# Three moves in the order of a chain of four residual layers: one weight split, half a product, the experts' product

## The chip, the cores and the metric

The kernel runs on one core of a Trainium2 chip. The metric is the device time of one execution in microseconds. Every execution launches the program once.

## What is computed

Four layers, each added to its input, on x of 64 batches x 32 rows x 512 numbers (2,048 rows of 512). Cut to what matters:

```python
# L0: gated MLP with an adapter of rank 16 chosen by batch
gate = x @ W_gate.T + 0.5 * (x @ A_gate[id].T) @ B_gate[id].T      # 512 -> 1376
up   = x @ W_up.T   + 0.5 * (x @ A_up[id].T)   @ B_up[id].T
act  = silu(gate) * up
x = x + act @ W_down.T + 0.5 * (act @ A_down[id].T) @ B_down[id].T # 1376 -> 512
# L1: rows of a batch mixed by a 32 x 32 matrix chosen by batch
x = x + einsum('bct,bcd->bdt', x, W1[cond])
# L2: a dense layer, and 8 experts of rank 16, the best two of each row weighted
base = x @ W.T
top2, ids = top_k(x @ Wr.T + 5 * one_hot(lang), 2)
gates = sum(one_hot(ids) * softmax(top2))
x = x + base + 2 * einsum('bter,bte,eor->bto', x @ A.T, gates, B)
# L3: as L1, with other matrices
x = x + einsum('bct,bcd->bdt', x, W3[cond])
```

## The kernel before

The 2,048 rows are 16 tiles of 128. Precision is kept by splitting: each float32 operand of a matmul is held as a high part (ScalarE casts it, `hi`) and a low part (VectorE subtracts the high part from the whole, `lo`, line 1126 for most of them), and `product` on TensorE makes three matmuls of each product: high by high, high by low, low by high (lines 1397 to 1399). A split thus passes ScalarE first and VectorE second. Both engines walk the same hand-written list, `lane_jobs`, in order; TensorE has its own hand-written order at the end of the program; SP and GpSimd issue transfers from their own lists. Semaphores tie the five together: a job's low part counts up `s_lo`, and TensorE waits for it.

**First half, L0.** It is worked in steps s = 0 to 47; a step is one tile i and one of three groups n of the 1,376 columns, and `ORDER` gives the first steps as (0,0), (0,1), (1,0), (0,2), (1,1), (1,2). A step has `gate(s)` and `up(s)` (four chunks of 128 input columns each, so twelve matmuls for 512 columns), then `adapters(s)`, which adds the adapter product and needs the split of step s's B: job `("b", s)`, tile `b_sel`. ScalarE and VectorE then form act (job `("gate", s)`); TensorE transposes it, it is split (job `("act", d)`, tile `act_hl`), and `down(d)` multiplies it by W_down. `down` of a tile's first group also needs the adapter matrices A for down, job `("adt", i)`, which go into the tile `wd_sb` beside W_down (jobs `("wd", f)`). B is gathered by GpSimd; before it loads the second group of W_down, SP waits until step 3's B has landed.

**Second half, L1 to L3.** Tile after tile, in the loop at the end of the TensorE program. `l2_base(i, 1)` and `l2_base(i, 0)` are the two halves of the product with W, Wr and the experts' A, twelve matmuls each, into the PSUM tile `l2_ps[i % 2]`. VectorE chooses the two experts (`route_top`, `route_weights`, `route_gates`, lines 1283 to 1306) and writes the weighted inner values `hg`. `transpose_hg(i - 1)` (line 1551) turns them, ScalarE and VectorE split them (`hgt_hl`, `s_hgtlo`), and `experts(i - 1)` adds their product with the experts' B to the base in `l2_ps[(i - 1) % 2]`, six matmuls of 256 columns. When it has ended (`s_l2`), ScalarE (`high_x3`, line 998) and VectorE (`low_x3`, line 1317) split the result into `x3_hl`. `l3(i - 2)` and `l1(i + 3)` are single products of other tiles. Since there are two `l2_ps` tiles, a tile's first product waits until the one before last is out:

```python
if t >= 2:
    pe.wait_ge(*((s_x3lo, t - 1) if t - 2 < PLAIN else x3_count(t - 2)))
    pe.wait_ge(s_hg, t - 1)
```

Up to t = 14 that is VectorE's `low_x3(t - 2)`; for t = 15 it is a copy on ScalarE. After `l3`, ScalarE copies its result (`copy_y`) and casts the next input of L1 (`high_x1`); GpSimd makes the low part of that (`low_x1`, line 862) for tiles up to 15. VectorE's `take_x2` ends a tile's work there and hands the tile after next to the DMA.

Of the kernel before, what the change touches and what calls it, by code (L numbers as in the profile page):

```python
# [49 lines left out]
HC = H // P  # L50
NT = ROWS // P
# [124 lines left out]
def wd_items(n):  # L176
    return [("wd", f) for f in pieces_of(n)]
# [47 lines left out]
def lane_jobs(s):  # L225

    if s <= FREE:
        w1u, w2g, w2u = wgu_items(1, 1), wgu_items(2, 0), wgu_items(2, 1)
        return {-1: first_items(),
                0: (wgu_items(1, 0) + [("at", 0)] + w1u[:2] + [("b", 0), w1u[2], ("tm", 0), w1u[3], ("t", 0), ("b", 1),
                    ("tc", 0), w2g[0], ("gate", 0), w2g[1], ("at", 1)]),
                1: w2g[2:] + [("gate", 1), ("tm", 1)] + w2u[:2] + [("t", 1)] + w2u[2:] + [("tc", 1)],
                2: [("b", 2), ("adt", 0), ("b", 3), ("adt", 1), ("gate", 2), ("act", 0)] + wd_items(0),
                3: [("gate", 3)] + wd_items(1) + [("act", 1), ("b", 4)],
                4: wd_items(2) + [("act", 2), ("gate", 4), ("bd", 0), ("b", 5), ("x", 2, 0)],  # L240
                5: [("tdm", 0), ("td", 0), ("act", 3), ("x1", 0), ("at", 2), ("gate", 5), ("b", 6)],
                6: [("act", 4), ("tm", 2), ("t", 2), ("adt", 2), ("gate", 6), ("b", 7)]}[s]
    i, n = divmod(s, NC)
    last = [("act", s - 1)] if s - 1 not in MOVED else []
    if i == NT:
        return last + [("bd", i - 1), ("tdm", i - 1), ("td", i - 1), ("x1", i - 1)]
    acts = ([("act", s - 2)] if s - 2 in MOVED else []) + last
    if n == 0:
        return [("tm", i)] + acts + [("t", i), ("gate", s), ("b", s + 1)]
    if n == 1:  # L250
        x = [("x", i + 1, 0)] if i + 1 < NT else []
        return acts + x + [("bd", i - 1), ("gate", s), ("tdm", i - 1), ("b", s + 1), ("td", i - 1)]
    jobs = acts[:1] + [("x1", i - 1)] + acts[1:]
    if i + 1 < NT:
        return jobs + [("at", i + 1), ("gate", s), ("b", s + 1), ("adt", i + 1)]
    return jobs + [("gate", s)]
# [6 lines left out]
def bass_conditioned_residual_chain(nc, x_t, x_rows, it_cond, it_lang, wgu, wd, a_all, a_gu, a_d, b_d,  # L263
# [6 lines left out]
    with ExitStack() as ctx:  # L270
# [54 lines left out]
        act = sb("act", [2, H], F32, mem_a)  # L325
# [1068 lines left out]
        def _(pe):  # L1394
# [22 lines left out]
            def gate(s, c0, c1):  # L1417
                i, n = ORDER[s]
                out_ = gate_of(s) if n or i < 2 else bank(s, 0)[:, 0:AW + GATE0]
                if c0 == 0 and slot_before(s) is not None:  # L1420
                    pe.wait_ge(s_mul, slot_before(s) + 1)
                if c0 == 0 and n == 0 and i >= 1:
                    pe.wait_ge(s_lo, s_lo_of(("x", i, 0)))
                if c0 == 0 and n == 0 and i >= 2:
                    pe.wait_ge(s_lo, s_lo_of(("at", i)))
                for c in range(c0, c1):
                    if i == 0:
                        pe.wait_ge(s_lo, s_lo_of(("wgu", n, 0, c)))
                        if n == 0 and c % 2 == 0:
                            pe.wait_ge(s_lo, s_lo_of(("x", 0, c // 2)))  # L1430
                    mm = product(out_, x_of(i, c), gate_moving(i, n, c), c == 0, False)
                if n == 0 and i >= 2 and c1 == HC:
                    mm.then_inc(s_tx, 1)
# [42 lines left out]
            def down(d):  # L1476
                i, n = divmod(d, NC)
                pe.wait_ge(s_lo, s_lo_of(("act", d)))
                if d == 0:
                    pe.wait_ge(s_mul, step_of(1, 0) + 1)  # L1480
                if n == 0:
                    pe.wait_ge(s_lo, s_lo_of(("adt", i)))
                    if i >= 1:
                        pe.wait_ge(s_x1, i)
                at = i % 2 * AD_HALF
                for j, f in enumerate(pieces_of(n)):
                    w = cw(f)
                    if i == 0:
                        pe.wait_ge(s_lo, s_lo_of(("wd", f)))
                    a_hl = [act_hl[0:w, d % 2, part, j, :] for part in range(2)]  # L1490
                    for half in range(2):
                        mm = product(down_ps[:, half, 0:D_COLS], a_hl,
                                     [wd_sb[0:w, f, part, half, at:at + D_COLS] for part in range(2)],
                                     n == 0 and j == 0, False)
                mm.then_inc(s_d, 1)
# [30 lines left out]
            def l2_base(t, half, c0=0, c1=HC):  # L1526

                if half == 1:
                    pe.wait_ge(s_x2tlo, t + 1)
                    if t == 0:  # L1530
                        pe.wait_ge(s_mul, STEPS)
                    if t == 1:
                        pe.wait_ge(s_x1, NT)
# [3 lines that stand above are left out]
                for c in range(c0, c1):  # L1537
                    if t == 0 and half == 1:
                        pe.wait_ge(s_wlo, c + 1)
                    x_hl = x2t_hl[:, t % 2, 0, c, :], x2t_hl[:, t % 2, 1, c, :]  # L1540
                    at, w = half * L2_WIDTH[0], L2_WIDTH[half]
                    mm = product(l2_ps[t % 2][:, half, 0:w], x_hl,
                                 [w2ra_hl[:, part, c, at:at + w] for part in range(2)], c == 0, c == HC - 1)
                if c1 == HC:
                    mm.then_inc((s_base, s_logits)[half], 1)
# [33 lines left out]
            def whole(part, s):  # L1579
                part(s, 0, HC)  # L1580
# [20 lines left out]
            adapters(2)  # L1601
            adapters(3)
            gate(4, HC // 2, HC)
            down(0)
            transpose_act(1)
            whole(up, 4)
            down(1)
            transpose_act(2)
            adapters(4)
# [13 lines left out]
            for s in range(FREE + 1, STEPS):  # L1623
                i, n = ORDER[s]
# [31 lines left out]
            l1(3)  # L1656
            for i in range(1, NT - 2):
                l2_base(i, 1)
                transpose_hg(i - 1)
                if i + 1 < MOVED_X2:  # L1660
                    transpose_x2(i + 1)
                l2_base(i, 0, 0, HC // 2)
                experts(i - 1)
                l2_base(i, 0, HC // 2, HC)
                if i >= 2:
                    l3(i - 2)
                if i + 3 < NT:
                    l1(i + 3)
            l2_base(NT - 2, 1)
            transpose_hg(NT - 3)  # L1670
            l2_base(NT - 2, 0, 0, HC // 2)
            experts(NT - 3)
            l2_base(NT - 2, 0, HC // 2, HC)
            l2_base(NT - 1, 1)
            transpose_hg(NT - 2)
            l3(NT - 4)
# [70 lines left out]
```

## Time and profile before

| | |
|---|---|
| median of 3 runs | 550.65 us (550.13 to 554.97) |
| the profiled execution | 551.23 us, of which its span 549.4 us |
| TensorE busy | 539.2 us, 98% of the span |
| VectorE, ScalarE, GpSimd busy | 60%, 38%, 39% |
| DMA | 105.71 MB, 192 GB/s in the mean |
| granted TensorE clock | 1.00 in the mean (2.4 GHz) |

Busy is the time in which an engine had an instruction at work, so the highest share shows the engine that all others feed. Matmuls overlap: each starts when the one before has given up the array, and its recorded duration reaches beyond the start of the next. The spacing of starts is therefore what a matmul costs, and "idle before" is counted from the end of the one before. The two halves of the program lie at about 6 to 450 us and 450 to 547 us of the span.

### The profile page before, as it was taken

The page shows a single profiled execution, that of the slowest core. Times are in us where ns is not written, and L with a number is a line of the kernel's source. Part 1 is how long each engine was busy: PE and PEld are TensorE (multiplying, and loading weights), DVE is VectorE, ACT ScalarE, POOL GpSimd, SP SyncE. Part 2 cuts the span into 40 slices and gives each one's busy share as a digit, 9 for nine tenths or more (in the row PEclk, how much of TensorE's full clock was granted, in tenths as well). Part 3 has the DMA queues.
Part 4 walks back from the last instruction along what each step waited for, and adds up shares of the span by engine and source line. Part 5 has one row for each costly group of instructions (what it writes and reads, how often), then busy time and mean ns, then how long its engine had stood idle before and what let it go on. Part 6 is the DMA issues. An engine that isn't in the chain of part 4 may idle for free.

```text
span 549.4 us, 8715 instructions
## 1 busy us (share of the span) xinstructions
PE 539.2 (98%) x3120; PEld 488.5 (89%) x3120; DVE 330.6 (60%) x775; ACT 209.7 (38%) x418; POOL 212.8 (39%) x236
## 2 busy tenths in 40 slices
PE   5999999999999999999999999999999999999997
PEld 5879989898989898989898989898989899999996
DVE  5788554645564646564555455545554577777765
ACT  6675242424242424242333323232323543444432
POOL 4743244746584757433232323241412342121100
PEclk9999999999999999999999999999999999999999
DMA  8985555666667666655555555564555832667642
GB/s 287 374 254 201 163 180 177 190 209 197 207 199 221 184 219 190 229 171 190 161 179 164 177 164 177 163 184 161 186 164 169 299 116 92 214 212 227 229 140 76
DMA packets 73466, 105.71 MB, mean 192 GB/s; under 512 B 9552, under 2 KB 40912, under 8 KB 73424
## 3 DMA queue, kind: packets, MB, share of 16 engines
q1 hardware_dynamic: 62400, 67.87, 37.6%
q0 software_dynamic: 10880, 37.23, 22.2%
q8 instruction: 24, 0.39, 0.3%
q14 instruction: 18, 0.15, 0.1%
q10 hardware_dynamic: 144, 0.06, 0.0%
HBM read 78.39 MB, written 26.74 MB: 191 GB/s over the span
## 4 chain that ended last, share of the span: by engine, by line
PE 96%; DVE 2%; DMA 1%; ACT 1%; issue 0%; SPq 0%; DVEq 0%; ACTq 0%
PE gu_ps L1397 15%; PE gu_ps L1399 15%; PE gu_ps L1398 15%; PE down_ps L1397 9%; PE down_ps L1398 9%; PE down_ps L1399 9%; PE l_ps L1397 5%; PE l_ps L1398 5%; PE l_ps L1399 5%; PE gu_ps L1404 3%; PE gu_ps L1405 3%; PE down_ps L1405 1%; PE down_ps L1404 1%; DMA wg_sb_raw<-wgu 1%; PE act_t L1473 0%; DVE wd_sb L1126 0%
## 5 line engine op out<-in xcount | busy, mean ns | idle before, releaser
L798 POOL DMA_INDIRECT b_sel_raw<-b_gu,idx_rank x48 | 46.3, 965 | 153.3 <-PE gu_ps L1405 135.2
L1397 PE MATMUL down_ps<-wd_sb,act_hl 128*128 128x288 f32 (+1 forms) x352 | 103.9, 295 | 0.3 <-DVE wd_sb L1126 0.3
L1398 PE MATMUL down_ps<-wd_sb,act_hl 128*128 128x288 f32 (+1 forms) x352 | 103.7, 295 | 0.0
L1399 PE MATMUL down_ps<-wd_sb,act_hl 128*128 128x288 f32 (+1 forms) x352 | 103.6, 294 | 0.0
L1397 PE MATMUL gu_ps<-w_sb,xt 128*128 128x512 f32 x256 | 101.1, 395 | 0.2 <-DVE act L1199 0.2
L1399 PE MATMUL gu_ps<-w_sb,xt 128*128 128x512 f32 x256 | 100.0, 391 | 0.0
L1398 PE MATMUL gu_ps<-w_sb,xt 128*128 128x512 f32 x256 | 100.0, 391 | 0.0
L1199 DVE TENSOR_TENSOR act<-act,gu_ps 128x512 f32<-128x512 f32 (+1 forms) x47 | 29.8, 634 | 106.7 <-ACT act L926 106.7
L926 ACT ACTIVATE act<-gu_ps 128x512 f32<-128x512 f32 (+1 forms) x47 | 26.2, 556 | 176.9 <-PE gu_ps L1405 176.9
L798 POOL DMA_INDIRECT a_raw<-a_all,idx_batch x60 | 70.2, 1170 | 54.0 <-DVE wd_sb L1126 39.9
L1397 PEld LDWEIGHTS down_ps<-wd_sb,act_hl 128*128 128x128 f32 (+1 forms) x352 | 66.0, 188 | 2.2 <-DVE wd_sb L1126 0.7
L1398 PEld LDWEIGHTS down_ps<-wd_sb,act_hl 128*128 128x128 f32 (+1 forms) x352 | 66.1, 188 | 1.2
L1399 PEld LDWEIGHTS down_ps<-wd_sb,act_hl 128*128 128x128 f32 (+1 forms) x352 | 66.0, 188 | 0.0
L1399 PEld LDWEIGHTS gu_ps<-w_sb,xt 128*128 128x128 f32 x256 | 48.1, 188 | 10.6
L1397 PEld LDWEIGHTS gu_ps<-w_sb,xt 128*128 128x128 f32 x256 | 48.1, 188 | 9.0 <-DVE act L1199 0.6
L1398 PEld LDWEIGHTS gu_ps<-w_sb,xt 128*128 128x128 f32 x256 | 48.2, 188 | 8.2
L1126 DVE TENSOR_TENSOR b_sel<-b_sel_raw,b_sel 128x1024 fp32r<-128x1024 f32 (+1 forms) x48 | 52.2, 1088 | 3.4 <-ACT b_sel L901 3.3
L862 POOL TENSOR_TENSOR x_hl<-x,x_hl 128x512 fp32r<-128x512 f32 x16 | 21.8, 1360 | 67.9 <-ACT x_hl L1032 67.9
L901 ACT CAST b_sel<-b_sel_raw 128x1024 fp32r<-128x1024 f32 (+1 forms) x48 | 45.7, 952 | 0.9 <-DMA b_sel_raw<-b_gu,idx_rank 0.9
L1397 PE MATMUL l_ps<-w2ra_hl,x2t_hl 128*128 128x328 f32 (+1 forms) x128 | 41.6, 325 | 0.0
L1398 PE MATMUL l_ps<-w2ra_hl,x2t_hl 128*128 128x328 f32 (+1 forms) x128 | 39.8, 311 | 0.0
L1399 PE MATMUL l_ps<-w2ra_hl,x2t_hl 128*128 128x328 f32 (+1 forms) x128 | 39.5, 309 | 0.0
(165 smaller groups left out, 1057.6 us busy)
## 6 DMA issues: line engine op xcount, KB each, us to landing
act_blocks<-act SPq DMA_DIRECT2D x41, 256.0 KB, 4.2
x_res<-act_blocks SPq DMA_DIRECT2D x164, 64.0 KB
xt_raw<-x_t SPq DMA_DIRECT2D x16, 256.0 KB, 5.0
w_sb_raw<-wgu SPq DMA_DIRECT2D x16, 256.0 KB, 7.9
x_res<-x_rows SPq DMA_DIRECT2D x16, 256.0 KB, 2.8
x_after_l<-x_res SPq DMA_DIRECT2D x16, 256.0 KB, 2.2
bd<-bd_hl SPq DMA_DIRECT2D x16, 256.0 KB
x<-x_after_l SPq DMA_DIRECT2D x16, 256.0 KB, 2.9
```

The lines of the kernel that those rows point to most:

```text
L798: nc.gpsimd.indirect_dma_start(out=dst, out_offset=None, in_=table, in_offset=bass.IndirectOffsetOnAxis(ap=idx, axis=0)).then_inc(s, 16)
L862: pool.tensor_tensor(x1_hl[:, t % 2, 1, :], x1[:, t % 2, :], x1_hl[:, t % 2, 0, :].bitcast(F32), ALU.subtract).then_inc(s_x1lo, 1)
L901: sc.copy(out_, in_).then_inc(s_hi, 1)
L926: sc.activation(act_of(s), gate_of(s), ACT.Silu).then_inc(s_silu, 1)
L1126: return ve.tensor_tensor(out_, raw, high.bitcast(F32), ALU.subtract)
L1199: ve.tensor_tensor(a, a, up_of(s), ALU.mult).then_inc(s_mul, 1)
L1397: pe.matmul(out_, stationary[0], moving[0], start=start, stop=False, skip_group_check=True)
L1398: pe.matmul(out_, stationary[0], moving[1], start=False, stop=False, skip_group_check=True)
L1399: return pe.matmul(out_, stationary[1], moving[0], start=False, stop=stop, skip_group_check=True)
L1404: pe.matmul(out_, stationary, moving[0], start=False, stop=False, skip_group_check=True)
L1405: return pe.matmul(out_, stationary, moving[1], start=False, stop=True, skip_group_check=True)
```

## The change

The arithmetic, the transfers and the number of instructions stay the same. Three orders change.

```diff
@@ lane_jobs @@
-                2: [("b", 2), ("adt", 0), ("b", 3), ("adt", 1), ("gate", 2), ("act", 0)] + wd_items(0),
+                2: [("b", 2), ("b", 3), ("adt", 0), ("adt", 1), ("gate", 2), ("act", 0)] + wd_items(0),
@@ the order on TensorE, first half @@
             gate(4, HC // 2, HC)
+            up(4, 0, HC // 2)
             down(0)
             transpose_act(1)
-            whole(up, 4)
+            up(4, HC // 2, HC)
             down(1)
@@ the order on TensorE, second half @@
             for i in range(1, NT - 2):
                 l2_base(i, 1)
+                l2_base(i, 0, 0, 1)
                 transpose_hg(i - 1)
                 if i + 1 < MOVED_X2:
                     transpose_x2(i + 1)
-                l2_base(i, 0, 0, HC // 2)
+                l2_base(i, 0, 1, HC)
                 experts(i - 1)
-                l2_base(i, 0, HC // 2, HC)
                 if i >= 2:
                     l3(i - 2)
                 if i + 3 < NT:
                     l1(i + 3)
             l2_base(NT - 2, 1)
+            l2_base(NT - 2, 0, 0, 1)
             transpose_hg(NT - 3)
-            l2_base(NT - 2, 0, 0, HC // 2)
+            l2_base(NT - 2, 0, 1, HC)
             experts(NT - 3)
-            l2_base(NT - 2, 0, HC // 2, HC)
```

On VectorE, in the work of step 2, around 34 us (`b_sel` of 704 columns is step 2's B, of 1024 columns step 3's; `wd_sb<-a_raw` is a tile's A for down, in two halves):

```order
 L1126 TENSOR_TENSOR b_sel<-b_sel_raw,b_sel 128x704 [waits s_hi]
-L1126 TENSOR_TENSOR wd_sb<-a_raw,wd_sb 128x11x32 [waits s_hi]
-L1126 TENSOR_TENSOR wd_sb<-a_raw,wd_sb 128x11x32
-L1126 TENSOR_TENSOR b_sel<-b_sel_raw,b_sel 128x1024 [waits s_hi]
+L1126 TENSOR_TENSOR b_sel<-b_sel_raw,b_sel 128x1024 [waits s_hi]
+L1126 TENSOR_TENSOR wd_sb<-a_raw,wd_sb 128x11x32 [waits s_hi]
+L1126 TENSOR_TENSOR wd_sb<-a_raw,wd_sb 128x11x32
```

Step 3's B now stands ahead of the first tile's A; ScalarE's casts stand likewise.

On TensorE, behind the last gate product of step 4, around 38 us (`gu_ps_1` is the up product, `down_ps` the down product of the first tile):

```order
 L1399 MATMUL gu_ps_0<-w_sb,xt 128x512
+L1397 MATMUL gu_ps_1<-w_sb,xt 128x512
+L1398 MATMUL gu_ps_1<-w_sb,xt 128x512
+L1399 MATMUL gu_ps_1<-w_sb,xt 128x512
+L1397 MATMUL gu_ps_1<-w_sb,xt 128x512
+L1398 MATMUL gu_ps_1<-w_sb,xt 128x512
+L1399 MATMUL gu_ps_1<-w_sb,xt 128x512
 L1397 MATMUL down_ps<-wd_sb,act_hl 128x288 [waits s_lo,s_mul]
```

The six up products are taken out behind the transpositions that follow the down product.

On TensorE, in a tile of the second half. Between the transposition of hg and the experts' product (`l_ps<-b_hl,hgt_hl`) two chunks of the base product stood before:

```order
 L1551 MATMUL hgt_ps<-ident_sb,hg 128x128
 L1397 MATMUL l_ps<-w2ra_hl,x2t_hl 128x320
 L1398 MATMUL l_ps<-w2ra_hl,x2t_hl 128x320
 L1399 MATMUL l_ps<-w2ra_hl,x2t_hl 128x320
 L1397 MATMUL l_ps<-w2ra_hl,x2t_hl 128x320
 L1398 MATMUL l_ps<-w2ra_hl,x2t_hl 128x320
 L1399 MATMUL l_ps<-w2ra_hl,x2t_hl 128x320
 L1397 MATMUL l_ps<-b_hl,hgt_hl 128x256
```

and now three:

```order
 L1551 MATMUL hgt_ps<-ident_sb,hg 128x128
 L1397 MATMUL l_ps<-w2ra_hl,x2t_hl 128x320
 L1398 MATMUL l_ps<-w2ra_hl,x2t_hl 128x320
 L1399 MATMUL l_ps<-w2ra_hl,x2t_hl 128x320
 L1397 MATMUL l_ps<-w2ra_hl,x2t_hl 128x320
 L1398 MATMUL l_ps<-w2ra_hl,x2t_hl 128x320
 L1399 MATMUL l_ps<-w2ra_hl,x2t_hl 128x320
 L1397 MATMUL l_ps<-w2ra_hl,x2t_hl 128x320
 L1398 MATMUL l_ps<-w2ra_hl,x2t_hl 128x320
 L1399 MATMUL l_ps<-w2ra_hl,x2t_hl 128x320
 L1397 MATMUL l_ps<-b_hl,hgt_hl 128x256
```

The first chunk of the half now stands ahead of the transposition, and the two chunks that followed the experts' product stand before it; behind the experts' product comes `l3(i - 2)` at once.

## Rows read from the trace of the kernel before

**Rows 1.** The page's first part: busy us, share of the span, instructions.
```profile
PE 539.2 (98%) x3120; PEld 488.5 (89%) x3120; DVE 330.6 (60%) x775; ACT 209.7 (38%) x418; POOL 212.8 (39%) x236
```

**Rows 2.** Timeline, TensorE, 35 to 44 us: start, duration, instruction [idle before <-releaser].
```profile
35.45 0.50 PE L1404 MATMUL gu_ps<-b_sel,t_hl 128*128 128x512 f32 x1 [0.74 <-DVE b_sel L1126]
...
37.63 0.39 PE L1399 MATMUL gu_ps<-w_sb,xt 128*128 128x512 f32 x1
38.29 0.37 PE L1397 MATMUL down_ps<-wd_sb,act_hl 128*128 128x288 f32 x1 [0.27 <-DVE wd_sb L1126]
...
41.10 0.48 PE L1397 MATMUL gu_ps<-w_sb,xt 128*128 128x512 f32 x1
...
43.93 0.29 PE L1397 MATMUL down_ps<-wd_sb,act_hl 128*128 128x288 f32 x1
```

**Rows 3.** Timeline, SP's transfers, ScalarE and VectorE, 32 to 43 us.
```profile
32.10 5.16 SPq L680 DMA_DIRECT2D wd_sb_raw<-wd  x8
...
32.31 0.87 ACT L905 CAST wd_sb<-a_raw 128x352 fp32r<-128x352 f32 x2
33.08 1.06 ACT L901 CAST b_sel<-b_sel_raw 128x1024 fp32r<-128x1024 f32 x1
...
33.25 0.96 DVE L1126 TENSOR_TENSOR wd_sb<-a_raw,wd_sb 128x352 fp32r<-128x352 f32 x2
34.17 1.23 DVE L1126 TENSOR_TENSOR b_sel<-b_sel_raw,b_sel 128x1024 fp32r<-128x1024 f32 x1
...
42.27 0.68 DVE L1126 TENSOR_TENSOR act_hl<-act_t,act_hl 128x512 fp32r<-128x512 f32 x1
```

**Rows 4.** Timeline, TensorE, a tile of the second half and the next's start.
```profile
469.15 0.31 PE L1397 MATMUL l_ps<-w2ra_hl,x2t_hl 128*128 128x328 f32 x1
...
470.95 0.27 PE L1551 MATMUL hgt_ps<-ident_sb,hg 128*128 128x128 f32 x1
...
471.94 0.35 PE L1397 MATMUL l_ps<-b_hl,hgt_hl 128*128 128x256 f32 x1
...
472.60 0.28 PE L1399 MATMUL l_ps<-b_hl,hgt_hl 128*128 128x256 f32 x1
472.72 0.31 PE L1397 MATMUL l_ps<-w2ra_hl,x2t_hl 128*128 128x320 f32 x1
...
473.61 0.39 PE L1397 MATMUL l_ps<-x_hl,bd_hl 128*128 128x512 f32 x1
...
474.99 0.31 PE L1397 MATMUL l_ps<-w2ra_hl,x2t_hl 128*128 128x328 f32 x1
```

**Rows 5.** Timeline, VectorE, the same tile: the subtraction that frees the bank.
```profile
473.60 0.69 DVE L1317 TENSOR_TENSOR x_hl<-l_ps,x_hl 128x512 fp32r<-128x512 f32 x1 [0.19 <-ACT x_hl L998]
```

**Rows 6.** Timeline, starts of tile 2 and of tile 14, the latter with its releaser.
```profile
462.83 0.39 PE L1397 MATMUL l_ps<-w2ra_hl,x2t_hl 128*128 128x328 f32 x1
...
532.04 0.69 DVE L1317 TENSOR_TENSOR x_hl<-l_ps,x_hl 128x512 fp32r<-128x512 f32 x1 [0.20 <-ACT x_hl L998]
...
532.84 0.39 PE L1397 MATMUL l_ps<-w2ra_hl,x2t_hl 128*128 128x328 f32 x1
```

**Rows 7.** Timeline, TensorE, the transposition of hg in tile 2.
```profile
465.05 0.33 PE L1551 MATMUL hgt_ps<-ident_sb,hg 128*128 128x128 f32 x1 [0.19 <-DVE hg L1306]
```

**Rows 8.** Timeline, VectorE's gate arithmetic and GpSimd's subtraction, tiles 2 and 3.
```profile
462.64 1.29 POOL L862 TENSOR_TENSOR x_hl<-x,x_hl 128x512 fp32r<-128x512 f32 x1 [5.64 <-ACT x_hl L1032]
463.02 0.92 DVE L1295 TENSOR_TENSOR route<-route 128x1 f32<-128x1 f32 x1
...
474.58 0.16 DVE L1295 TENSOR_TENSOR route<-route 128x1 f32<-128x1 f32 x1
...
475.30 0.17 DVE L1302 TENSOR_TENSOR route<-route 128x8 f32<-128x8 f32 x1
475.50 0.29 DVE L1306 TENSOR_TENSOR hg<-l_ps,route 128x128 f32<-128x128 f32 x1
...
475.69 1.30 POOL L862 TENSOR_TENSOR x_hl<-x,x_hl 128x512 fp32r<-128x512 f32 x1 [4.38 <-ACT x_hl L1032]
```

## Prediction

> **What bounds the kernel now.** I read the page first: TensorE is busy for 539.2 of 549.4 us [rows 1]. Nearly all that is not busy lies before the first product and in the tail, so the rest of the work was read in two narrow stretches of the timeline, for each of which I noted at what time a product starts, what it waited for, and when the result it needs was there.
>
> The first stretch is 34 to 44 us. TensorE waits 0.74 us at 35.45 for step 3's B [rows 2]; VectorE's subtraction of that B runs from 34.17 for 1.23 us, to 35.40 [rows 3], so the adapter products start 0.05 after it. At 38.29 the first down product waits for a piece of W_down [rows 2]. The second stretch is the last 100 us, the sixteen tiles of the second half. Call the start of a tile's first product (`l2_base(i, 1)`) S. In an ordinary tile S is 469.15 and the next tile's is 474.99: 5.84 us [rows 4]. TensorE has no idle time there, but it has little slack either. That start needs a PSUM bank which the tile before last left: experts(i-1) ends, ScalarE casts the bank (`high_x3`), VectorE subtracts (`low_x3`, line 1317), and only then `s_x3lo` lets `l2_base(i+1, 1)` begin. The last of the six experts products starts at 472.60 [rows 4], the subtraction 1.00 later at 473.60, and it takes 0.69, to 474.29 [rows 5]. So the bank is free 0.70 us ahead of 474.99.
>
> How long TensorE needs after a release is seen where it comes last. The subtraction at 532.04 ends at 532.73 and the product starts at 532.84, 0.11 later, and takes 0.39 where its like takes 0.31 at 469.15 [rows 4, 6]; so 0.11 and then about 0.07 more. The second tile's start at 462.83 is of the same kind (0.39) [rows 6]: no slack at all there.
>
> **The change in the first stage.** Nothing is added or removed; two items trade places on ScalarE and VectorE, and six of the twelve up products of step 4 go ahead of down(0).
>
> B ahead of A: step 3's B has landed by 32.10, where SP's wait for it ends [rows 3]. ScalarE is free for its cast at 32.31, where it casts A now; the cast takes 1.06, to 33.37. VectorE is free at 33.25 and subtracts from 33.41 to 34.64. The adapters start at 34.69 instead of 35.45: 0.76 gained. The work behind on VectorE is the same in sum, but starts 0.11 later for the wait on the cast.
>
> Half an up product ahead of down(0): the last gate product before it starts at 37.63, its slot ends 0.23 later at 37.86; minus 0.76 is 37.10. Twelve up products take 2.83 (41.10 to 43.93) [rows 2], six 1.38. So down(0) can start at 38.48, and its weights, there for 38.29 now and 0.11 later then, are in time. From down(0) to down(1) it is 5.64 now; less the 0.08 of a restart and the six products that is 4.18, so down(1) could start at 42.66. But down(1) also needs the activations' low part: VectorE's subtraction at 42.27 takes 0.68 [rows 3], to 42.95, with the 0.11 to 43.06. TensorE starts at 43.17 in place of 43.93, and loses 0.08 on the first product. **Gain 0.68.** The wait has moved from B and W_down to the activations, where VectorE's queue, which nothing shortens, is the bound. The ends: 0 if the B isn't there early, 1.27 (43.93 - 42.66) if the activations were no bound. I take 0.68, since VectorE is unbroken there. After 44 us TensorE has all its inputs early, so this gain is kept.
>
> **The change in the second stage.** Experts(i-1) goes behind all twelve products of `l2_base(i, 0)`, and the transposition of hg behind the first three. What each tile has afterwards, from S:
> - `l2_base(i, 1)`: 1.80 (469.15 to 470.95), plus 0.07 if S was a restart
> - three products: 0.44 (six take 0.89, 472.72 to 473.61)
> - transposition: 0.10 (470.95 to 471.94 is 0.99, less the six products' 0.89)
> - nine products: 1.33
> - to the start of the last experts product: 0.59 (five spacings of 0.12). Now it is 0.66 (471.94 to 472.60), since the first experts product just meets its operand; with nine products between, this 0.07 goes.
>
> All from [rows 4]. The last experts product thus starts at S + 4.33 instead of S + 3.45. To this come 1.00, 0.69 and 0.11 [rows 5, 6]: the next S cannot be before S + 6.13. TensorE's own work is 5.84 - 0.07 + 0.07 = 5.84, so a wait of 0.29 us stands where there was 0.70 of slack. This is **+0.29 for each of the ten starts** of tiles 4 to 13: +2.9.
>
> Other starts, one by one. Tile 2 (462.83) has no slack, six products go in front of its releaser: +0.89. Tile 3: TensorE waited 0.19 there for hg (465.05) [rows 7] and the tile lasted 6.32 (462.83 to 469.15); now 6.13: -0.19. Tile 14 (532.84), before which no `l1` stands, is at its release already: +0.88. Tile 15 has neither `l1` nor `l3` in front of it; its releaser is ScalarE's copy; I price it as tile 14, +0.88. Behind it the tail is as before. **Sum of the stage: 2.9 + 0.89 - 0.19 + 0.88 + 0.88 = +5.36.**
>
> Who else is moved? GpSimd. ScalarE's copy of y and cast of x1 follow `l3`, and GpSimd's subtraction follows them. `l3` starts at 473.61, GpSimd at 475.69 [rows 4, 8], 2.08 later, and takes 1.30. Call the start of the last experts product L. Now `l3` is at L + 0.12, so GpSimd runs from L + 2.20 to L + 3.50. VectorE's gate arithmetic follows the bank's subtraction (L + 1.00): line 1295 stands 0.98 behind it (474.58), so L + 1.98 to 2.14, just ahead of GpSimd; line 1302 (475.30) at L + 2.70, in the middle of it; hg (475.50) 0.20 after that [rows 8]. In the trace an operation of VectorE that meets GpSimd is held to its end: line 1295 at 463.02 takes 0.92 instead of 0.16 and ends at 463.94, GpSimd's ends at 463.93 [rows 8]. So line 1302 is held to L + 3.50, and hg is there at L + 3.70 + 0.29 = L + 3.99. The next transposition wants it at L + 1.80 + 1.87 + 0.44 = L + 4.11. It just fits: cost nothing, cover 0.12.
>
> The Trainium skill (SBUF — State Buffer, Who interferes with whom) says that a VectorE instruction with two SBUF inputs contends with a GpSimd instruction that reads SBUF, and the row at 463.02 agrees (0.92 against 0.16 us). It says further that copies, casts and `tensor_scalar` can take the shared ports too. No row here shows that for a wide one. By that the two operations between lines 1295 and 1302 would be held as well, and the cover of 0.12 would be gone: that is the second rival below.
>
> **Sum.** -0.68 + 5.36 = +4.68. The profiled execution took 551.23 us (span 549.4); it would be 555.9 and its span 554.1. The median of the three runs is 550.65, 0.58 lower: **555.3**.
>
> **The rivals.**
> 1. The release isn't late (other side). Everything does what was meant: -0.68, the 0.19 of the wait on hg, 0.07 in twelve tiles: -1.7, 548.9 us. It decides where the bank is free by the time TensorE wants it: experts end 0.82 later against a slack of 0.70, so the ScalarE-VectorE chain would have to be 0.12 to 0.29 shorter than the 1.69 that it shows [rows 4, 5], and at tiles 2, 14 and 15 even 0.9 shorter. Against it: these durations repeat from tile to tile. 0.06.
> 2. VectorE is held longer by GpSimd, so hg becomes the bound. If line 1295 is caught (it clears by 0.06), the transposition comes as at 465.05, 1.12 after GpSimd's end at 463.93 [rows 7, 8], at L + 4.62 against L + 4.11: 0.51 for each of the nine tiles in which GpSimd still subtracts, +4.6, 559.9 us. If only the `tensor_scalar` operations are, half: +2.3, 557.6. For it: margins of 0.06 and 0.12; against it: the distances are fixed by the same release. 0.16.
> 3. B isn't there at 32.31. It landed only 0.2 before [rows 3]. If it comes 0.8 later the gain of the first stage is gone: +5.36, 556.0 us. 0.10.
>
> **How the numbers follow.** Mine holds 0.68, at 554.3 to 556.4 by itself: 0.08, the price of one restart, either way at each of the thirteen starts. The range takes in the third rival and the milder form of the second: 553.0 to 558.0; outside are the first (0.06), the full form of the second (0.07) and a rest. One per cent, 5.5 us, is about what a measurement of this kernel can tell from no change. Over 556.2 lie the second rival (0.16), some of the third and of mine (0.12 together): slower 0.28. Under 545.1 nothing leads; TensorE is at work 98% of the span [rows 1]: 0.02. Same: 0.70.
>
> **What would show it.** In the timeline after: adapters of step 3 at 34.7 without idle, down(0) at 38.5, and a wait of down(1) on VectorE's `act_hl` of some 0.3 to 0.5. In the table of waits a new row at the top, TensorE `l_ps` L1397 waiting for VectorE `x_hl` L1317, in 13 tiles, some 0.1 to 0.9 each, and tiles 6.13 apart instead of 5.84. Line 1302 at about 1 us instead of 0.17. Were TensorE to wait for hg (L1306) at line 1551 instead, the second rival is right; were there no wait in the second stage, the first. My sum is wrong if the chain from experts to the release is not the 1.80 of now, or if a tile's x2 blocks, which VectorE now hands to the DMA later in a tile, come too late.

## The result, and the profile after

The changed kernel took **558.29 us** (median of ten executions, 557.59 to 561.92), against 555.25 us for the kernel before (ten executions, 550.13 to 556.76) in the same comparison: a ratio of **1.0097, interval 1.0063 to 1.0132**. The prediction was 555.3 us in a range of 553.0 to 558.0, so the time lies 0.3 us above the range. The 555.25 needs a remark: four of its ten executions lie at 550 to 552 us and six at 555 to 557 us, while in three later comparisons the median of before was 551.25, 552.02 and 551.57 us. Against those the change costs 6.3 to 7.0 us (1.1 to 1.3%), though they ran at other times and on three different chips. What can make one execution 4 us longer than the next is found at the end, in the trace of e7_mid. Executions over 1.5% above the quickest of the same kernel (one of e9_mid_release took 1085.72 us) are in the medians and not in the ratios.

The profiled execution took 557.59 us, its span is 555.8 us (before 549.4). The page's first line of TensorE, which answers to [rows 1], and its chain that ended last:

```profile
PE 542.3 (98%) x3120; PEld 486.2 (87%) x3120; DVE 340.1 (61%) x775; ACT 210.7 (38%) x418; POOL 209.8 (38%) x236
...
PE 87%; DVE 4%; POOL 3%; DMA 3%; issue 2%; ACT 1%; SPq 0%; ACTq 0%; DVEq 0%
```

VectorE is busy 9.5 us more (340.1 against 330.6) with the same 775 instructions. There aren't more of them, so some must have become longer. That is the first sign that GpSimd stands in VectorE's way.

I noted the start S of each tile's first product (128x328) in both traces; the difference from one tile to the next:

| stretch into tile | before, us | after, us | difference | forecast |
|---|---|---|---|---|
| 2 | 5.59 | 6.48 | +0.89 | +0.89 |
| 3 | 6.32 | 6.07 | -0.25 | -0.19 |
| 4 to 12 (nine) | 5.84 to 5.85 | 6.29 to 6.46 | +4.77 in sum | +2.6 |
| 13 | 5.84 | 6.13 | +0.29 | +0.29 |
| 14 | 5.25 | 6.13 | +0.88 | +0.88 |
| 15 | 4.53 | 5.33 | +0.80 | +0.88 |
| tile 1 to tile 15 | 80.13 | 87.51 | **+7.38** | +5.36 |

Tile 1 itself starts 1.02 us earlier than before (456.22 against 457.24), and 7.38 - 1.02 = 6.36 is the growth of the span but for 0.04.

The timeline of TensorE after, a tile and the next one's start, answers to [rows 4]:

```profile
468.77 0.39 PE L1397 MATMUL l_ps<-w2ra_hl,x2t_hl 128*128 128x328 f32 x1
...
471.19 0.33 PE L1551 MATMUL hgt_ps<-ident_sb,hg 128*128 128x128 f32 x1
...
472.68 0.28 PE L1397 MATMUL l_ps<-b_hl,hgt_hl 128*128 128x256 f32 x1
...
473.27 0.28 PE L1399 MATMUL l_ps<-b_hl,hgt_hl 128*128 128x256 f32 x1
473.39 0.40 PE L1397 MATMUL l_ps<-x_hl,bd_hl 128*128 128x512 f32 x1
...
475.06 0.39 PE L1397 MATMUL l_ps<-w2ra_hl,x2t_hl 128*128 128x328 f32 x1
```

The last experts product starts at S + 4.50 (forecast 4.33), and `l3` 0.12 behind it. ScalarE and VectorE free the bank as before; these rows answer to [rows 5]:

```profile
473.65 0.58 ACT L998 CAST x_hl<-l_ps 128x512 fp32r<-128x512 f32 x1 [0.80 <-PE l_ps L1399]
474.26 0.69 DVE L1317 TENSOR_TENSOR x_hl<-l_ps,x_hl 128x512 fp32r<-128x512 f32 x1 [0.57 <-ACT x_hl L998]
```

From 473.27 to 474.26 it is 0.99, the subtraction ends at 474.95, and TensorE starts 0.11 later at 475.06: the release chain of the forecast (1.00 + 0.69 + 0.11), to 0.01 us. The start itself is a restart (0.39 instead of 0.31). What is new is the 0.17 ahead of it: the transposition of hg at 471.19 takes 0.33, the mark of a late operand. The waits of TensorE after say the same (engine, output, line, releaser: us in total, times, longest):

```profile
PEld l_ps L1397 <- issue: 7.7, 13, 1.2
...
PEld hgt_ps L1551 <- DVE hg L1306: 2.5, 9, 0.4
...
PE l_ps L1397 <- issue: 1.8, 3, 0.8
```

The wait for the bank stands where it was forecast, but the table puts it down to "issue", not to the subtraction of line 1317. Of the thirteen in the first row twelve are starts of tiles 2 to 9 and 11 to 14, and one is tile 1, which waits 0.21 us before the change too; tile 10 is in the third row. It has to be seen by the times themselves: in each of tiles 2 to 14 the start is 0.10 or 0.11 behind the subtraction's end. And nine transpositions wait for hg, which was forecast for none.

Why hg is late, in the tile that starts at 468.77 and in a later one:

```profile
468.79 0.62 ACT L1032 CAST x_hl<-x 128x512 fp32r<-128x512 f32 x1 [0.16 <-DMA x<-x_after_l]
...
469.35 0.29 DVE L1301 TENSOR_SCALAR route<-head_sb,route 128x8 f32<-128x8 f32 x1
...
469.49 1.30 POOL L862 TENSOR_TENSOR x_hl<-x,x_hl 128x512 fp32r<-128x512 f32 x1 [5.74 <-ACT x_hl L1032]
469.67 1.14 DVE L1302 TENSOR_TENSOR route<-route 128x8 f32<-128x8 f32 x1
470.84 0.29 DVE L1306 TENSOR_TENSOR hg<-l_ps,route 128x128 f32<-128x128 f32 x1
...
481.93 1.36 DVE L1301 TENSOR_SCALAR route<-head_sb,route 128x8 f32<-128x8 f32 x1
481.98 1.29 POOL L862 TENSOR_TENSOR x_hl<-x,x_hl 128x512 fp32r<-128x512 f32 x1 [4.90 <-ACT x_hl L1032]
```

GpSimd's subtraction and VectorE's gate arithmetic now lie on top of each other. At 469.67 it is line 1302 that is held (1.14 us, before 0.17 in [rows 8]); at 481.93 it is line 1301, a `tensor_scalar` of 128x8 (1.36 us instead of 0.29). Both end 0.02 us after GpSimd's instruction; the one at 463.02 in [rows 8] ended 0.01 after it. Of the nine tiles three have line 1302 held (the next start 6.29 to 6.32 us on) and six line 1301 (6.37 to 6.46).

In the first half, after, the rows that answer to [rows 2, 3]:

```profile
31.98 1.05 ACT L901 CAST b_sel<-b_sel_raw 128x1024 fp32r<-128x1024 f32 x1 [0.42 <-DMA b_sel_raw<-b_gu,idx_rank]
33.07 1.23 DVE L1126 TENSOR_TENSOR b_sel<-b_sel_raw,b_sel 128x1024 fp32r<-128x1024 f32 x1 [0.58 <-ACT b_sel L901]
34.35 0.51 PE L1404 MATMUL gu_ps<-b_sel,t_hl 128*128 128x512 f32 x1 [0.48 <-DVE b_sel L1126]
...
42.79 0.40 PE L1397 MATMUL down_ps<-wd_sb,act_hl 128*128 128x288 f32 x1 [0.28 <-DVE act_hl L1126]
```

The wait has moved to `act_hl` at down(1), as forecast, and down(1) starts 1.14 us earlier than before. Most of that is not the change's doing (below).

### The profile page after: what moved, and what is told of

It is laid out like the page before. It is cut to its first block, busy times and chain, and to the rows that moved or that the text cites. A ratio compares the mean times of both kernels' runs of the same rounds, so it can differ in the third digit from the quotient of the medians.

```text
span 555.8 us, 8715 instructions
## 1 busy us (share of the span) xinstructions
PE 542.3 (98%) x3120; PEld 486.2 (87%) x3120; DVE 340.1 (61%) x775; ACT 210.7 (38%) x418; POOL 209.8 (38%) x236
## 4 chain that ended last, share of the span: by engine, by line
PE 87%; DVE 4%; POOL 3%; DMA 3%; issue 2%; ACT 1%; SPq 0%; ACTq 0%; DVEq 0%
PE gu_ps L1397 13%; PE gu_ps L1399 13%; PE gu_ps L1398 13%; PE down_ps L1397 8%; PE down_ps L1398 8%; PE down_ps L1399 8%; PE l_ps L1397 5%; PE l_ps L1398 4%; PE l_ps L1399 4%; PE gu_ps L1404 3%; PE gu_ps L1405 3%; POOL a_raw L798 2%; DVE wd_sb L1126 1%; DMA b_sel_raw<-b_gu,idx_rank 1%; DMA x_landed<-x_blocks 1%
## 5 line engine op out<-in xcount | busy, mean ns | idle before, releaser
L798 POOL DMA_INDIRECT a_raw<-a_all,idx_batch x60 | 68.6, 1144 | 54.0 <-DVE wd_sb L1126 39.6
```

Source lines behind the costliest of these rows:

```text
L798: nc.gpsimd.indirect_dma_start(out=dst, out_offset=None, in_=table, in_offset=bass.IndirectOffsetOnAxis(ap=idx, axis=0)).then_inc(s, 16)
```

## The experiments

For each profile the time from the start of tile 1 to that of tile 15 is given, since it is free of what happens in the first half; before the change it is 80.13 us. The ratios are against the kernel before, run beside on the same chip.

**e1_first: only the two moves in the first half.**

```diff
-                2: [("b", 2), ("adt", 0), ("b", 3), ("adt", 1), ...
+                2: [("b", 2), ("b", 3), ("adt", 0), ("adt", 1), ...
+            up(4, 0, HC // 2)
             down(0)
             transpose_act(1)
-            whole(up, 4)
+            up(4, HC // 2, HC)
```

> Only the two moves of the first half (step 3's B split ahead of the first tile's A; half of step 4's up product ahead of the first down); second half as before. My account: both traces show TensorE waiting for B (0.74 us before, 0.48 after, B's DMA landing 0.42 late for ScalarE after) and the rest of the gain is 0.2 to 0.7 us, so this kernel is 0.2 to 0.7 us faster than before and nothing in the second half moves (tile starts 5.84 apart). Rival: the first half's moves cost something (DMA or queue effects), and the kernel is slower than before by 0.5 us or more.

Measured: 552.06 us, ratio 1.0014 [0.9972, 1.0056]. Tile 0 starts at 446.74 instead of 447.36, 0.62 earlier. The adapters of step 3 start at 34.66 (forecast 34.69) and down(0) at 38.42 (38.48), neither with an idle time before it in the record, and down(1) starts at 43.16 (43.17), with the wait that was named:

```profile
43.16 0.40 PE L1397 MATMUL down_ps<-wd_sb,act_hl 128*128 128x288 f32 x1 [0.29 <-DVE act_hl L1126]
```

The tiles of the second half stand 5.84 and 5.85 apart as before; tile 1 to 15 is 80.09. So the first half does what its step says, by 0.6 to 0.7 us in the trace. The times can't confirm it: the median is 0.8 us higher than that of before, and the interval is 4.6 us wide.

**e2_second: only the move of the experts' product and the transposition**, with the first half as before (the loop as in the diff of the change).

> Only the second half's move (first chunk ahead of the transposition of hg, experts behind all base products); first half as before. My account: the whole loss is here: +7 us from the second tile's start on against a trace of before (6.13 apart without GpSimd's meeting, 6.3 to 6.45 with it), so 6 to 8 us slower than a quick run of before. Rival: the first half carries part of the loss; then this kernel is less than 4 us slower than e1_first.

Measured: 560.17 us, ratio 1.0150 [1.0098, 1.0202]. Tile 1 to 15 took 88.25 us, +8.12. It is this part that costs. Against the 551.25 us of before the median is 8.9 us higher, where 6 to 8 were expected; three of its six executions lie at 558.2 to 558.4 and three at 561.9 to 564.6, and the profiled one, 561.93, has a wait of 2.01 us in the first half. The second half is 0.7 us worse than in the full change, and half of that is one tile, which took 6.78 us (the same tile in the full change 6.42):

```profile
515.16 0.62 ACT L982 CAST x2t_hl<-x_landed 128x512 fp32r<-128x512 f32 x1 [1.56 <-DMA x_landed<-x_blocks]
...
515.79 0.57 ACT L998 CAST x_hl<-l_ps 128x512 fp32r<-128x512 f32 x1
...
516.50 0.68 DVE L1317 TENSOR_TENSOR x_hl<-l_ps,x_hl 128x512 fp32r<-128x512 f32 x1
...
517.28 0.39 PE L1397 MATMUL l_ps<-w2ra_hl,x2t_hl 128*128 128x328 f32 x1 [0.55 <-issue]
517.44 1.29 POOL L862 TENSOR_TENSOR x_hl<-x,x_hl 128x512 fp32r<-128x512 f32 x1 [5.07 <-ACT x_hl L1032]
517.47 1.27 DVE L1295 TENSOR_TENSOR route<-route 128x1 f32<-128x1 f32 x1
```

The last experts product starts at 515.06. ScalarE waits 1.56 us for the DMA of x2, the cast that begins the release is queued behind that one, and the subtraction starts 1.44 us after the last experts product instead of 0.99. The last two rows show line 1295 held whole by GpSimd, the case which the forecast saw clear by 0.06 us. Behind tile 2, where it is held before the change too, this happens once, and the tile that it delays (517.28 to 523.72) took 6.44 us, no more than those with line 1301 held.

**e3_poollate: the changed kernel, with GpSimd's subtraction held back until hg is written.** Nothing else moves; VectorE's gates then never meet it.

```diff
             def low_x1(t):
                 pool.wait_ge(s_x1hi, t + 1)
+                if t >= 5:
+                    pool.wait_ge(s_hg, t - 3)
```

> The changed kernel, with GpSimd's subtraction of x1 (low_x1, tiles 5 to 15) held until the tile's hg is written, so that it can't meet VectorE's gate arithmetic. Theory A (VectorE held by GpSimd makes hg late in ten tiles): lines 1301 and 1302 fall back to 0.2 to 0.3 us, tiles 3 to 13 are 6.13 apart throughout, and the kernel is 2.0 to 2.2 us faster than the changed one. Theory B (only the bank's release counts; the extra over 6.13 has another cause, such as late x2 blocks from the DMA): the gate lines become short but the spacing stays 6.3 to 6.45, time unchanged within 0.5.

Measured: 556.04 us, ratio 1.0074 [1.0042, 1.0106]; span 554.1 us, tile 1 to 15 85.23 us. Every tile from 4 to 14 now stands 6.11 to 6.13 us from the one before. The rows of a tile:

```profile
469.61 0.28 DVE L1303 TENSOR_SCALAR route<-head_sb,route 128x8 f32<-128x8 f32 x1
469.93 0.17 DVE L1304 TENSOR_TENSOR route<-route 128x8 f32<-128x8 f32 x1
470.13 0.29 DVE L1308 TENSOR_TENSOR hg<-l_ps,route 128x128 f32<-128x128 f32 x1
...
470.56 1.28 POOL L864 TENSOR_TENSOR x_hl<-x,x_hl 128x512 fp32r<-128x512 f32 x1 [4.77 <-DVE hg L1308]
```

(The edit shifts the line numbers by two.) Line 1302, here 1304, takes its 0.17 us again. Without the meeting tile 1 to 15 is thus 87.51 - 85.23 = **2.28 us** shorter. In the changed kernel 2.16 of these lie ahead of the last experts product, where hg is waited for; 0.12 is one release (at 513.36) behind a late DMA of x2, which in e3_poollate comes in time. What is left over before, 85.23 - 80.13 = 5.10 us, is put down to the bank; the early release below tests it.

**e4_same: the kernel before, once more**, for the spread.

> The kernel before, unchanged, to see its own spread and a second trace of it: its ten runs lie in two groups, near 551 and near 556 us. If the groups are a matter of the order of events within the kernel, a trace near 556 shows tiles of the second half over 5.84 apart or waits that the first trace has not; if they come from outside (the moment at which TensorE's clock rises, the chip), the tiles are 5.84 apart and the time sits elsewhere.

Measured: 551.33 us (550.49 to 557.66), ratio 1.0005 [0.9973, 1.0037]. Its second half repeats to 0.01 us a tile (tile 3 to 0.05), tile 1 to 15 in 80.09. What this execution took more, 1.0 us, lies in the first half: a down product waits 1.28 us for `act_hl` at 185.84, where the trace of [rows 1] has no such wait. It isn't one of the executions near 556 us, so it says nothing of those.

**e5_release: the changed kernel, with the bank given back early.** VectorE copies the finished base from PSUM to SBUF (`x3`) in one instruction, this alone releases the bank, and ScalarE and VectorE make the high and low parts from the copy. It adds an instruction of 0.68 us to each tile and takes the cast and the subtraction out of TensorE's way. GpSimd is left as in the changed kernel.

```diff
+            def raw_x3(t):
+                ve.wait_ge(s_l2, t + 1)
+                ve.tensor_copy(halves(x3[:, t % 3, :], 0, H), base_of(t, 0, H)).then_inc(s_x3raw, 1)
...
-                low_x3(i - 1)
+                raw_x3(i - 1)
                 route_weights(i)
                 route_gates(i)
+                low_x3(i - 1)
...
-                        pe.wait_ge(*((s_x3lo, t - 1) if t - 2 < PLAIN else x3_count(t - 2)))
+                        pe.wait_ge(*((s_x3raw, t - 1) if t - 2 < PLAIN else x3_count(t - 2)))
```

> The changed kernel, with the bank let go earlier: VectorE first copies the tile's result from PSUM to SBUF, TensorE's next product in the bank waits for that copy alone, and ScalarE and VectorE split it from SBUF (VectorE's subtraction behind hg); one VectorE copy more per tile. GpSimd's subtraction stays where it is. Bank theory: the bank is free 1.1 us after the start of the last experts product instead of 1.8, TensorE's own work (5.77) is the bound, tiles 3 to 13 are 5.77 to 5.8 apart, hg is written before GpSimd starts, and the kernel takes 549.5 to 550.5, 8 us less than the changed one and 0.5 to 1.5 less than before. Rival (the order itself is slow, by hg or by the x2 blocks): the spacing stays at 6.1 or more and at least 4 us of the loss remain.

Measured: 553.41 us, ratio 1.0024 [0.9984, 1.0063]; the profiled execution 550.67 us with a span of 548.5. The 549.5 to 550.5 us that were expected are missed: six executions lie at 550.7 to 552.7 and six at 554.1 and more. The tiles up to 13 now stand 5.76 to 5.87 us apart (one 6.05), and tile 1 to 15 took 80.70 us, 6.81 less than the changed kernel. A tile's start, with the copy and GpSimd of this kernel:

```profile
478.22 0.68 DVE L1318 COPY x<-l_ps 128x512 f32<-128x512 f32 x1
...
479.10 0.39 PE L1405 MATMUL l_ps<-x_hl,bd_hl 128*128 128x512 f32 x1
479.32 0.31 PE L1403 MATMUL l_ps<-w2ra_hl,x2t_hl 128*128 128x328 f32 x1
```

The bank is free at 478.90 and wanted at 479.32; the product takes 0.31 again, no restart. The same edit also ends the meeting with GpSimd, in every tile: VectorE's gates now start right behind the 0.68 us copy, without the 0.6 us for ScalarE's cast, and hg has begun before GpSimd starts. So this run alone doesn't separate the two; e3_poollate and e6_release_poollate do. Tile 15, whose releaser is ScalarE's copy and not in the edit, stays at 5.33.

**e8_before_release: the kernel before, with the same early release.** The control.

> The kernel before, with the early release of the bank of e5_release and nothing else. Control: before has 0.70 us of slack at that wait, so by the bank theory the spacing stays at 5.84 and only the starts of tiles 2 and 14, which are at their release, gain about 0.1 each: same time as before within 0.5 us. If this is faster by over 1 us, e5_release proves nothing of the order.

Measured: 551.39 us, ratio 1.0004 [0.9966, 1.0043], most tiles 5.84 us apart (two of 5.98 and 6.04), tile 1 to 15 80.29. Where the release isn't the bound, giving it earlier brings nothing. The 6.8 us of e5_release are therefore the cure of what the change had made, and no gain of the early release itself.

**e6_release_poollate: the changed kernel with both cures.**

> The changed kernel with both cures: the bank released by VectorE's copy to SBUF, and GpSimd's subtraction held back behind hg. With the early release alone the tiles started 5.76 to 5.87 us apart. If the 0.09 us that some tiles kept came from GpSimd holding a gate line, they now start 5.76 us apart throughout, about 0.5 us less in sum: 550.5 us in an undisturbed execution, a ratio of 0.999 to 1.002. If the spread comes from something else (the base product's own late operand, or VectorE's copy ahead of the gates), the spacing stays mixed and the time with it.

Measured: 551.76 us, ratio 1.0008 [0.9974, 1.0041]; tile 1 to 15 80.66 us. From e3_poollate it differs by the early release alone, and takes 85.23 - 80.66 = **4.57 us** less: with GpSimd out of the way in both, this is what the late release costs, and the late DMA of one tile (below) hides another 0.46.

What was expected against e5_release is not shown. GpSimd starts 0.58 us behind hg in both (in e5_release 474.86 behind 474.28, here 475.75 behind 475.17), so holding it back there changed nothing. Ten of the eleven starts of tiles 3 to 13 stand 5.76 to 5.84 apart and one 6.23. In that one a DMA is late, ScalarE's cast of x2 with it, and VectorE's copy that frees the bank is queued behind its own part of that split:

```profile
507.42 0.62 ACT L985 CAST x2t_hl<-x_landed 128x512 fp32r<-128x512 f32 x1 [1.30 <-DMA x_landed<-x_blocks]
...
508.14 0.69 DVE L1264 TENSOR_TENSOR x2t_hl<-x_landed,x2t_hl 128x512 fp32r<-128x512 f32 x1 [0.87 <-ACT x2t_hl L985]
508.75 0.68 DVE L1320 COPY x<-l_ps 128x512 f32<-128x512 f32 x1
```

The copy starts 1.17 us after the last experts product instead of 0.34. It is the same in e5_release: in two tiles (5.85 and 5.87) the copy starts 0.80 and 0.82 after it, and three that begin with such a restart take 5.83 to 5.85. Once the release is early there is little slack towards that DMA.

**e7_mid: the experts' product behind three of the four chunks** (in tiles 1, 13 and 14 where it was before), with GpSimd held back and the first-half moves. The release chain starts three products (0.44 us) earlier than in the change.

```diff
+                first = 0 if i in (1, NT - 3) else 1
-                l2_base(i, 0, 0, 1)
+                l2_base(i, 0, 0, first)
                 transpose_hg(i - 1)
...
-                l2_base(i, 0, 1, HC)
+                l2_base(i, 0, first, 2 + first)
                 experts(i - 1)
+                l2_base(i, 0, 2 + first, HC)
```

> A compromise: the changed kernel with experts one chunk earlier (behind three of the four chunks), in tiles 1, 13 and 14 where it was before the change, and GpSimd's subtraction held until hg is written. By the bank theory the bank is free at 5.61 of a tile whose own work takes 5.77, so there is no wait: tiles 3 to 12 are 5.77 to 5.8 apart, and the kernel is 0.5 to 1.5 us faster than before, near 550.2. If a start needs more lead than 0.16 us the spacing is 5.84 and the kernel equals before.

Measured: 552.60 us, ratio 0.9993 [0.9957, 1.0028]. Most tiles stand 5.83 to 5.84 us apart, 5.24 and 4.53 at the end, 79.64 from tile 1 to 15: 0.49 less than before, 0.39 of it in tile 3. By moving back one chunk the whole loss is gone, but the 5.77 us per tile that were hoped for are not there.

**e9_mid_release: e7_mid with the early release.**

> This kernel puts together what the runs so far gave room for: both moves in the first half; the experts behind three of the four chunks of the base products (in tiles 1, 13 and 14 where they stood before); GpSimd's subtraction held back behind hg; and the PSUM bank of the base products given back by one VectorE copy to SBUF. If the 0.07 to 0.08 us that the order with three chunks kept (its tiles started 5.83 us apart) is the late release of the bank, the tiles now start 5.76 us apart, as most did with the early release, and the last two stretches stay at 5.24 and 4.53 us: about 79 us from the second tile's start to the last one's, 1.1 us under the kernel before, and 0.6 us less in the first half, so 549.5 us, a ratio of 0.997. If the 5.83 us come from something that the release doesn't touch (hg's transposition or the chain over line 1317), the spacing stays at 5.83 and the time at 550.5 us or within 0.2% of before.

Measured: 552.78 us, ratio 1.0022 [0.9988, 1.0056]. The spacing stays at 5.82 to 5.85 (two of 5.92), tile 1 to 15 in 79.51, and TensorE waits 1.07 us for step 3's B in this trace; the 549.5 us that were hoped for are missed. So the 0.07 over e5's 5.76 is not the release. The rows of TensorE in e9_mid_release say what it is:

```profile
482.11 0.27 PE L1559 MATMUL hgt_ps<-ident_sb,hg 128*128 128x128 f32 x1
...
483.10 0.35 PE L1405 MATMUL l_ps<-b_hl,hgt_hl 128*128 128x256 f32 x1
...
485.71 0.31 PE L1405 MATMUL l_ps<-w2ra_hl,x2t_hl 128*128 128x328 f32 x1
```

Between the transposition and the first experts product stand six products, as in [rows 4], and the experts' operand just comes in time: 0.35 as at 471.94 there. With nine products between, as in the changed kernel at 472.68, the same product takes 0.28. These are the 0.07 us per tile which the change does gain. They would come to 0.8 us of 551. e5_release keeps them and pays 1.22 us at the starts of tiles 2, 14 and 15 (5.87, 5.39 and 5.33 against 5.59, 5.25 and 4.53). Its order with the old one in tiles 1, 13 and 14 was not tried. None of the kernels beats the one before by an amount that the times can tell.

## Why the prediction was wrong, step by step

**The late release: right, in place and size.** "The next S cannot be before S + 6.13": 6.13 us into tiles 13 and 14 of the changed kernel, and 6.11 to 6.13 into all from 4 to 14 in e3_poollate. In the stretch into 14 GpSimd no longer subtracts; in the one into 13 it still does, but comes too late to hold anything:

```profile
527.05 0.17 DVE L1302 TENSOR_TENSOR route<-route 128x8 f32<-128x8 f32 x1
527.07 1.31 POOL L862 TENSOR_TENSOR x_hl<-x,x_hl 128x512 fp32r<-128x512 f32 x1 [5.20 <-ACT x_hl L1032]
```

e3_poollate against e6_release_poollate (4.57 us), with e8_before_release as the control, shows that it is this wait. The single starts were off by -0.06 (tile 3) and -0.08 (tile 15, whose releaser is ScalarE's copy and which I had priced as tile 14).

**"It just fits: cost nothing, cover 0.12": this step failed.** It cost 2.28 us (e3_poollate against the changed kernel), because the term that places GpSimd was wrong. GpSimd was put at L + 2.20, by its distance from `l3` in one row of before. With L = 473.27 it starts at 475.77, L + 2.50:

```profile
475.07 0.62 ACT L1032 CAST x_hl<-x 128x512 fp32r<-128x512 f32 x1 [0.20 <-DMA x<-x_after_l]
...
475.77 1.31 POOL L862 TENSOR_TENSOR x_hl<-x,x_hl 128x512 fp32r<-128x512 f32 x1 [4.98 <-ACT x_hl L1032]
475.96 1.14 DVE L1302 TENSOR_TENSOR route<-route 128x8 f32<-128x8 f32 x1
```

In the nine tiles with a meeting GpSimd starts at L + 2.28 to L + 2.58. ScalarE's cast ahead of it waits for the DMA that brings x; the record shows 0.16 to 0.23 us of it in three of the nine tiles and names nothing in the others. The one trace of before that the prediction had shows that wait nowhere, so no row had a price for it: the distance was carried over to a place where another input came last. e4_same, the kernel before once more, has one (0.26 us at 470.51); a second trace would have warned. The load of x is issued 0.43 us behind the transfer of VectorE's `take_x2`, which stands behind hg. Before, it was issued at 470.98 for a cast at 474.98, 4.00 us ahead; after, at 472.22 for the cast at 475.07, 2.85 ahead. By these rows a late hg makes the next load late, and with it GpSimd and the next hg; no run separates that.

Two smaller errors of the working nearly cancel. Line 1302's hand-over to hg was taken as 0.20 from its end, but in [rows 8] 0.20 is the distance of the two starts (475.30 and 475.50), and 0.03 that from the end: 0.17 too much. And from the end of hg to the transposition it takes 0.06 (471.13 to 471.19), which the cover left out. With both put right the cover would have been 0.23; GpSimd's 0.30 ate it. hg starts at 477.14 and is there at 477.43, L + 4.16 and not L + 3.99. In the tile that starts at 468.77 the transposition was wanted at S + 2.31 (1.87 and 0.44), 471.08; it starts at 471.19, 0.11 late, and its own restart makes the 0.17 by which the last experts product is behind S + 4.33.

The further error is the one that was named as open: the narrow `tensor_scalar` of line 1301 is held too (1.36 us), which makes tiles of 6.37 to 6.46 out of 6.29. That is the second rival in its milder form, 557.6 us with a chance inside 0.16. That the profiled execution took 557.59 is luck to the digit: the half in that rival was a guess, three of the nine tiles had line 1302 held, and not 1301, and the first half was off by 0.34. A cover of 0.12 us between two sums was no ground for five chances in six on "nothing".

**The first half: right in mechanism, with luck in the sum.** e1_first gives 43.16 for the forecast 43.17 and 0.62 us at tile 0. In the changed kernel's own trace step 3's B was 0.42 late (the third rival, partly), and TensorE was nonetheless 1.02 us ahead at tile 1. That is luck. It had been 0.85 ahead before the first changed instruction, which leaves 0.17 for the change in this trace and not 0.68: its first products stood 0.29 us apart until about 9 us of the span and 0.16 from there on, in the trace of before only from about 11 us. The same program does both.

**The sum.** The second half cost 2.02 more than forecast and the first half took 0.34 less: +1.68, which is the profiled 557.59 against my 555.9. The other 1.3 us up to 558.29 lie in the last step, "the median of the three runs is 0.58 lower": of the ten executions of the changed kernel the profiled one is the lowest, so subtracting went the wrong way (0.70 us up instead of 0.58 down).

**The chances.** "Slower by over 1%" had 0.28. The ratio in the first comparison is 1.0097; against the 551.25 us that before took beside the experiments it would be 1.013. With the failed step's 2.3 us the sum would have been 557.6, 1.3% above before, and that chance the larger one.

## What to carry to other kernels

Moving a product behind independent work gives its operand more time and takes it from whoever waits for its result: before the move, follow the result to the next use of its PSUM bank, and subtract the delay from the slack that is there (0.88 us later, against a slack of 0.70 less the 0.11 of a restart, cost 0.29 us in each of ten tiles). Where a step is found to fit by a tenth of a microsecond next to an engine that blocks another, put the failure's price into the sum and not into the rivals. And a distance between two instructions holds only as long as the same input comes last; whether it is read from start to start or from end to start has to stand beside it.

## What the runs showed of the hardware

**Who holds whom.** These VectorE instructions, with all their operands in SBUF, met GpSimd's subtraction and ended with it: 0.17 became 1.14 us (128x8 `tensor_tensor`), 0.29 became 1.36 (128x8 `tensor_scalar`), 0.16 became 1.27 (128x1 `tensor_tensor`), from the rows above. The `tensor_scalar` was held though it had started 0.05 us before GpSimd; the `tensor_tensor` at 527.05, 0.02 us before it, was not. The Trainium skill (SBUF — State Buffer, Who interferes with whom) has the `tensor_scalar` among those that can take shared ports; the row at 481.93 agrees, and also for one of eight columns. Not held was a `tensor_scalar` of one column, in the trace of before, inside GpSimd's 462.64 to 463.93 of [rows 8]:

```profile
462.65 0.14 DVE L1293 TENSOR_SCALAR route<-route 128x1 f32<-128x1 f32 x1
```

The other way round, GpSimd pays: where a wide subtraction of VectorE had begun before it, in e9_mid_release, VectorE keeps its 0.68 us and GpSimd takes 1.45 instead of 1.30:

```profile
480.75 0.68 DVE L1324 TENSOR_TENSOR x_hl<-x,x_hl 128x512 fp32r<-128x512 f32 x1
481.12 1.45 POOL L865 TENSOR_TENSOR x_hl<-x,x_hl 128x512 fp32r<-128x512 f32 x1 [4.37 <-ACT x_hl L1035]
```

**A late DMA, and the clock behind it.** e7_mid's profiled execution took 554.14 us, while its lowest five took 549.4 to 550.5. Its trace shows where:

```profile
130.52 0.40 ACT L1023 CAST bd_hl<-bd_raw 128x256 fp32r<-128x256 f32 x1 [5.90 <-DMA bd<-bd_hl]
130.83 0.61 ACT L903 CAST act_hl<-x_res 128x512 fp32r<-128x512 f32 x1
...
132.33 0.61 PE L1399 MATMUL down_ps<-wd_sb,act_hl 128*128 128x288 f32 x1 [2.77 <-DVE act_hl L1128]
132.74 0.44 PE L1400 MATMUL down_ps<-wd_sb,act_hl 128*128 128x288 f32 x1
132.98 0.44 PE L1401 MATMUL down_ps<-wd_sb,act_hl 128*128 128x288 f32 x1
```

ScalarE stands 5.90 us for a DMA (`bd`), the cast of the activations is queued behind it, and TensorE waits 2.77 us. Then the granted clock is 0.50 (1.2 GHz) in the stretch from 132.5 to 135.4, and the first spacing is 0.41 us (0.24 after the wait in e4_same) and the next twelve are 0.24 instead of 0.13: 1.4 us more. Together 4.2 us. The columns of the stretches are the busy us (instructions) of PE, PEld, DVE, ACT and POOL, then PEclk, DMA share and GB/s:

```profile
129.00:132.50 3.50, 0.73 (x4) 0.31 (x3) 1.02 (x2) 1.98 (x5) 1.45 (x2) 0.95 0.32 124
132.50:135.40 2.90, 2.90 (x13) 2.90 (x14) 2.63 (x4) 1.41 (x2) 2.52 (x3) 0.50 0.42 132
```

After the waits of 1.28 us (e4_same) and 2.01 us (e2_second) for the same tile (`act_hl`) the products stood 0.13 apart at once and the granted clock stayed at 1.00. One such wait in the first half is thus about the 4 us by which the longer executions of a kernel lie above the shorter ones. Only this one of the longer executions with a low clock was traced, so their cause is not shown, but the granted clocks on record fit: beside the experiments the kernel before was executed 81 times; 17 of these have a mean granted clock of 0.997 or less, and all have spans of 552.3 us or more; of the other 64 all but two have spans of 552.0 or less. A stretch of 2.9 us at half the clock is what brings the mean of 552 us to 0.997.
